# Attention scores that contract over one head's 64 rows, in a macaron block (MoE, attention, MoE) on one core

## The chip, the core and the metric

The kernel runs on one core of one Trainium2 chip. The core has five engines that run their own instruction streams and meet at semaphores: PE (TensorE, matmuls; its weight loads are shown apart as PEld), DVE (VectorE), ACT (ScalarE), POOL (GpSimd) and SP (SyncE, which here only issues DMAs). The metric is the device time of one execution in microseconds (us).

## What is computed

The reference, cut to what matters here:

```python
x = x + 0.5 * ffn(layernorm(x))       # mixture of 8 experts, 2 per token
x = x + attention(layernorm(x))
x = x + 0.5 * ffn(layernorm(x))       # the same weights again

def attention(h):                      # h: 4 x 512 x 256, 16 heads of 16 columns
    q, k, v = split(h @ w_qkv.T)
    scores = q @ k.T / sqrt(16)                        # per batch and head: 512 x 512
    scores = where(causal, scores, finfo.min)
    return (softmax(scores) @ v) @ w_o.T
```

The change touches the attention alone, and the tables that its causal masks read.

## The kernel before

The program is three phases in a row, `feed_forward` ("first"), `attention` and `feed_forward` ("second"), each with its own block of five hand-written instruction streams. The change is in `attention` and in `Constants.fill`, which POOL runs at the very start.

**Units.** Attention works in 8 units: 4 batches times 2 halves of 8 heads (`UNIT_HEADS`). `unit_loop` runs `front` for the first unit alone, and then 8 `step`s. In each step one unit's exponentials and values are made (`key_scores`, `exps`, `values`), and beside them the front of the next unit: its projections (`project`), the transposes that make its stacks (`turn`), and its scores for the row maxima (`scores`, `maximum`). The list `BESIDE` says by hand which part of the next unit's front stands behind which of the 16 `key_scores` calls (8 heads, two halves each); `VALUES_AFTER`, `OUTPUTS_AFTER` and `PROJECT_AFTER` place the rest. The last step has no next unit, so it has no scores.

**Stacks.** To reach float32 accuracy with fast matmuls, each head's q and k are split into a high and a low part and stacked: one head takes 64 contraction rows (three products of 16 rows, and two rows for the maximum). A transpose of 128 x 128 turns two heads at once, so a pair of heads lies in `q_stack` one above the other: the even head in partitions 0 to 63, the odd head in 64 to 127. A matmul here always reads all 128 partitions. So that the other head of the pair adds nothing, `k_stack` has two copies of the key columns (its second index, 0 or 1), each with the other head's half zero. The zeros are written once by POOL (L925); ACT copies each transposed block in two instructions of 64 partitions (`turn`, L986), one into each copy.

**Scores.** `scores` (PE, L1261) makes the queries-by-keys scores of one query tile. Query tiles 0 and 1 take two neighbouring heads in one bank (`SCORES`), tiles 2 and 3 one head. Each score matmul is followed by a bfloat16 matmul of 128 columns that adds the causal mask to the diagonal block: identity times `hide_later` (L1263). DVE then reduces the bank to row maxima (L1091 for two heads, L1095 for one). `key_scores` (L1289) makes the transposed scores that ACT's exponential reads (L1000); only the unit's last head has mask matmuls there (L1291), the others are cleared by POOL after the exponential.

**Banks and waits.** `project`, `turn` and `scores` share three PSUM banks in turn (`use`); a use waits until DVE or ACT has read the one three before it. The first `key_scores` of a step waits for a DMA that writes the maxima into `q_stack` (`max_in`). `values` (L1306) multiplies into 32 output partitions at a time: four matmuls on four column blocks of the array.

Of the kernel before, what the change touches and what calls it, by code (L numbers as in the profile page):

```python
# [47 lines left out]
class Constants:  # L48


    def __init__(self, nc, enter):
        def sb(name, shape, dtype=F32):
            return enter(nc.sbuf_tensor(name, shape, dtype))

        self.identity = sb("identity", [P, P])
        self.identity_bf = sb("identity_bf", [P, P], BF16)
        self.earlier = sb("earlier", [P, P], BF16)
        self.ones = sb("ones", [P, P], BF16)
        self.lane = sb("lane", [P, P])
# [5 lines left out]
        self.hide_later = sb("hide_later", [P, P], BF16)  # L65
        self.hide_later_t = sb("hide_later_t", [P, P], BF16)

        self.filled = enter(nc.semaphore("filled"))
        self.ready = enter(nc.semaphore("tables_ready"))

    def fill(self, pool):

        for table, value in ((self.identity, 0.0), (self.identity_bf, 0.0), (self.earlier, 1.0), (self.ones, 1.0),
                             (self.not_first, 1.0), (self.hide_later, 0.0), (self.hide_later_t, 0.0)):
            pool.memset(table[:], value).then_inc(self.filled, 1)
# [7 lines left out]
        pool.wait_ge(self.filled, 12)  # L83
        for table in (self.identity, self.identity_bf):
# [12 lines left out]
        pool.wait_ge(self.filled, 18)  # L97
# [578 lines left out]
def attention(nc, const, x, stats, x_rows, out_rows, w_qkv, w_o, rows_stored):  # L676
# [27 lines left out]
    SCORES = [(qt, (h, h + 1)) for qt in (0, 1) for h in range(0, UNIT_HEADS, 2)]  # L704
# [54 lines left out]
    with ExitStack() as stack:  # L759
# [13 lines left out]
        k_stack = [sb(f"k_stack{i}", [P, 2, PAIRS, SEQ], F32R) for i in range(2)]  # L773
# [138 lines left out]
        def _(pool):  # L912
# [11 lines left out]
            for i in range(2):  # L924
                pool.memset(k_stack[i][:].rearrange("p a b c -> p (a b c)").bitcast(F32), 0.0).then_inc(k_ready, 1)  # L925
# [30 lines left out]
        def _(act):  # L956
# [23 lines left out]
            def turn(u, hh, t):  # L980
# [66 lines left out]
        def _(v):  # L1047
# [38 lines left out]
            def maximum(u, hh, n):  # L1086
# [3 lines left out]
                if len(heads) == 2:  # L1090
                    v.reduce_max(maxima[:, qt, :, heads[0] // 2],  # L1091
# [94 lines left out]
        def _(pe):  # L1186
# [62 lines left out]
            def scores(u, hh, n):  # L1249
# [30 lines left out]
            def key_scores(b, hh, i):  # L1280

                h, half = i // 2, i % 2
                q, k = q_stack[hh][:, h // 2, :], k_stack[hh][:, h % 2, h // 2, :]
                pe.wait_ge(exped, 2 * UNIT_HEADS * (2 * b + hh) + i + 1)
                for j, (kt, q0) in enumerate(KEY_TILES[2 * half:2 * half + 2]):
# [4 lines left out]
                    if here:  # L1290
                        last = pe.matmul(out[:, kt * P - q0:(kt + 1) * P - q0], const.identity_bf[:], const.hide_later_t[:],  # L1291
                                         start=False, stop=True)
# [127 lines left out]
```

## Time and profile before

| | us |
|---|---|
| median of 3 runs | 1012.59 |
| the three runs | 1010.59, 1012.59, 1016.1 |
| span of the profiled execution | 1011.8 |
| PE busy, of the span | 836.9 |
| attention, from its first transposes to its last output matmuls | about 348 to 672 on the span's clock |

The time of the profiled execution is given as its span, from the first to the last instruction; it lies 0.8 us under the median of the runs. Rows of a timeline give the start, the duration, the engine, the line, the operation, output <- inputs, the shape and the count of merged instructions. The end of a matmul (start plus duration) is modelled with its pipeline, so that two ends in a row tell how far apart two matmuls really finish. A row "x2" merges two.

### The profile page before, as it was taken

How to read it: one execution, taken by the hardware profiler on the slowest of the kernel's cores; microseconds unless marked ns; L12 is line 12 of the kernel's file. 1: busy time of each engine (PE TensorE's matmuls, PEld its weight loads, DVE VectorE, ACT ScalarE, POOL GpSimd, SP SyncE). 2: the span in 40 equal slices, each digit the busy share in tenths (PEclk: the TensorE clock that was granted, in tenths of full speed). 3: DMA queues.
4: the chain of work that ended last, by engine and by line, in shares of the span. 5: the costliest groups of instructions: out<-in, count | busy, mean ns of one | idle time of the engine just before them, and what ended most of it. 6: DMA issues, size and time to landing. Idle time of an engine off the chain costs nothing. (4 is left out here: it accounts for less than half of the span.)

```text
span 1011.8 us, 16585 instructions
## 1 busy us (share of the span) xinstructions
PE 836.9 (83%) x5884; PEld 736.3 (73%) x5884; DVE 493.9 (49%) x1038; ACT 413.6 (41%) x743; POOL 308.5 (30%) x388
## 2 busy tenths in 40 slices
PE   4459899889898167999999999854599898998993
PEld 2459899889897155777677667442499898998993
DVE  7734444344341377655775666245554244433530
ACT  3024444344342132665465555523054344433530
POOL 1162543444333500211221121100533345335232
PEclk9779899999999578999999999777799899998997
DMA  9053234423411400101102001022133442443211
GB/s 332 1 162 95 58 105 108 119 48 103 117 22 17 151 1 2 42 3 44 44 0 80 6 1 41 2 86 102 52 121 99 120 113 49 109 119 94 47 16 20
DMA packets 52553, 72.15 MB, mean 71 GB/s; under 512 B 6272, under 2 KB 44160, under 8 KB 52480
## 3 DMA queue, kind: packets, MB, share of 16 engines
q1 hardware_dynamic: 37152, 52.71, 15.3%
q0 software_dynamic: 15360, 18.90, 10.7%
q8 instruction: 25, 0.41, 0.2%
q14 instruction: 16, 0.13, 0.0%
HBM read 53.49 MB, written 18.87 MB: 72 GB/s over the span
## 5 line engine op out<-in xcount | busy, mean ns | idle before, releaser
L1000 ACT ACTIVATE at_probs<-at_ps_keys 128x896 f32<-128x896 f32 (+1 forms) x128 | 96.0, 759 | 86.7 <-PE at_ps_keys L1289 77.4
L561 DVE SCALAR_TENSOR_TENSOR second_h_lo<-second_ps_h,second_h_hi 128x320 fp32r<-128x320 f32 x128 | 62.9, 491 | 103.9 <-ACT second_h_hi L414 103.9
L561 DVE SCALAR_TENSOR_TENSOR first_h_lo<-first_ps_h,first_h_hi 128x320 fp32r<-128x320 f32 x128 | 62.9, 491 | 103.2 <-ACT first_h_hi L414 103.2
L660 PE MATMUL second_ps_o<-second_w_hi,second_h_hi 128*128 128x256 f32 x320 | 95.8, 299 | 17.2 <-ACT second_scaled L407 17.2
L340 POOL DMA_INDIRECT out_dram<-second_scaled,second_add_now x40 | 63.8, 1594 | 151.1 <-DMA out_dram<-second_scaled,second_add_now 105.2
L340 POOL DMA_INDIRECT after_first<-first_scaled,first_add_now x40 | 63.7, 1593 | 146.8 <-DMA after_first<-first_scaled,first_add_now 104.4
L660 PE MATMUL first_ps_o<-first_w_hi,first_h_hi 128*128 128x256 f32 x320 | 95.7, 299 | 14.6 <-ACT first_scaled L407 14.6
L660 PE MATMUL second_ps_o<-second_w_lo,second_h_hi 128*128 128x256 f32 x320 | 93.7, 293 | 0.0
L660 PE MATMUL first_ps_o<-first_w_lo,first_h_hi 128*128 128x256 f32 x320 | 93.7, 293 | 0.0
L660 PE MATMUL second_ps_o<-second_w_hi,second_h_lo 128*128 128x256 f32 x320 | 93.6, 293 | 0.0
L660 PE MATMUL first_ps_o<-first_w_hi,first_h_lo 128*128 128x256 f32 x320 | 93.5, 292 | 0.0
L1261 PE MATMUL at_ps<-at_k_stack,at_q_stack 128*128 128x256 f32 (+2 forms) x256 | 84.5, 398 | 2.6 <-ACT at_k_stack L986 1.4
L1289 PE MATMUL at_ps_keys<-at_q_stack,at_k_stack 128*128 128x256 f32 (+2 forms) x256 | 76.7, 386 | 11.0 <-DMA at_q_stack<-at_max_t 9.5
L414 ACT ACTIVATE second_h_hi<-second_ps_h 128x320 fp32r<-128x320 f32 x128 | 56.0, 437 | 60.0 <-PE second_ps_h L649 60.0
L414 ACT ACTIVATE first_h_hi<-first_ps_h 128x320 fp32r<-128x320 f32 x128 | 55.9, 437 | 59.5 <-PE first_ps_h L649 59.5
L1095 DVE TENSOR_REDUCE at_maxima<-at_ps 128x1 f32<-128x512 f32 (+1 forms) x128 | 71.8, 617 | 16.8 <-PE at_ps L1263 16.4
L660 PEld LDWEIGHTS second_ps_o<-second_w_hi,second_h_hi 128*128 128x128 f32 x320 | 64.9, 203 | 18.2 <-ACT second_scaled L407 18.2
L660 PEld LDWEIGHTS first_ps_o<-first_w_hi,first_h_hi 128*128 128x128 f32 x320 | 64.7, 202 | 15.6 <-ACT first_scaled L407 15.6
L943 POOL TENSOR_SCALAR_AFFINE_SELECT at_probs<-at_probs 128x512 f32<-128x512 f32 (+1 forms) x64 | 35.3, 577 | 127.7 <-ACT at_probs L1000 127.7
L1289 PEld LDWEIGHTS at_ps_keys<-at_q_stack,at_k_stack 128*128 128x128 f32 x256 | 43.2, 203 | 32.7 <-ACT at_probs L1000 16.0
L660 PEld LDWEIGHTS second_ps_o<-second_w_lo,second_h_hi 128*128 128x128 f32 x320 | 64.9, 203 | 0.0
L660 PEld LDWEIGHTS first_ps_o<-first_w_lo,first_h_hi 128*128 128x128 f32 x320 | 64.8, 203 | 0.0
(266 smaller groups left out, 2033.1 us busy)
## 6 DMA issues: line engine op xcount, KB each, us to landing
first_w_raw<-in_L_ffn_w_dram SPq DMA_DIRECT2D x16, 1024.0 KB, 8.0
second_w_raw<-in_L_ffn_w_dram SPq DMA_DIRECT2D x16, 1024.0 KB, 6.7
at_xt<-at_xt_all SPq DMA_DIRECT2D x3, 1024.0 KB, 4.8
x<-_attn_hidden_states_dram SPq DMA_DIRECT2D x4, 512.0 KB, 5.8
normed_rows<-first_xn SPq DMA_DIRECT2D x4, 512.0 KB, 6.7
x<-after_first SPq DMA_DIRECT2D x4, 512.0 KB, 7.2
at_x_now<-after_first SPq DMA_DIRECT2D x4, 512.0 KB, 5.2
out_dram<-x SPq DMA_DIRECT2D x4, 512.0 KB, 3.2
```

Of the source, the lines that this page charges most:

```text
L340: pool.indirect_dma_start(sum_rows, bass.IndirectOffsetOnAxis(ap=add_now[par][:, s:s + 1], axis=0), scaled[par][:, s, :], None, bounds_che ...
L414: act.activation(h_hi[:, f, a * HALF:(a + 1) * HALF], ps_h[:, f % 2, a, 0:HALF], ACT.Relu).then_inc(h_hi_done, 1)
L561: v.scalar_tensor_tensor(h_lo[:, f, a * HALF:(a + 1) * HALF], ps_h[:, f % 2, a, 0:HALF], 0.0, h_hi[:, f, a * HALF:(a + 1) * HALF].bitcast( ...
L660: last = pe.matmul(ps_o[:, (par + s) % 2, 0:D], h[:, f, cs], w[par][:, f, :], start=(f == 0 and n == 0), stop=(f == FT - 1 and n == 2))
L943: pool.affine_select(probs[g][:, 0:heads, at:at + P], probs[g][:, 0:heads, at:at + P], [[0, heads], [1, P]], ALU.is_ge, 0.0, base=0, chann ...
L1000: act.activation(probs[h // GROUP][:, h % GROUP, columns], keys_columns(half), ACT.Exp, scale=float(HD) ** -0.5).then_inc(exped, 1)
L1095: v.reduce_max(maxima[:, qt, h % 2, h // 2:h // 2 + 1], bank[:, 0:(qt + 1) * P], AX_X).then_inc(front_kept, 1)
L1261: pe.matmul(out, q_stack[hh][:, h // 2, qt * P:(qt + 1) * P], k_stack[hh][:, h % 2, h // 2, 0:keys], start=True, stop=False)
L1289: last = pe.matmul(out, k[:, kt * P:(kt + 1) * P], q[:, q0:SEQ], start=True, stop=not here)
```

## The change

- `k_stack` loses its second index: the even head's keys stand in partitions 0 to 63 and the odd head's in 64 to 127, as in `q_stack`. ACT fills it with one copy of 128 partitions (`turn`) in place of two of 64. POOL's clearing writes 2048 columns in place of 4096.
- Score and key-score matmuls name the head's 64 partitions of both operands. In the built program they have a tile of [64, 128] of the array, at row 0 or row 64; before, they had [128, 128]. The columns that stream through are as many as before.
- A mask is two bfloat16 matmuls with 64 contraction rows, on the same rows as the head: `pick` and `hide_half` (`hide_half_t` for the key scores), each half of what the identity and the mask table did. The tables are filled at the start by 12 selects of 64 partitions in place of 2 of 128, and 3 memsets in place of 2.
- Where two heads share a bank, they are now of the same parity (0 and 2, 1 and 3, ...).

```diff
-                             (self.not_first, 1.0), (self.hide_later, 0.0), (self.hide_later_t, 0.0)):
+                             (self.not_first, 1.0), (self.pick, 0.0), (self.hide_half, 0.0), (self.hide_half_t, 0.0)):
...
-        pool.affine_select(self.hide_later[:], self.hide_later[:], [[-1, P]], ALU.is_ge, NEG, base=0,
-                           channel_multiplier=1).then_inc(self.filled, 1)
-        pool.affine_select(self.hide_later_t[:], self.hide_later_t[:], [[1, P]], ALU.is_ge, NEG, base=0,
-                           channel_multiplier=-1).then_inc(self.filled, 1)
+        HALF_ROWS = P // 2
+        for half in range(2):
+            rows = slice(half * HALF_ROWS, (half + 1) * HALF_ROWS)
+            pool.wait_ge(self.filled, 17 + 6 * half)
+            for part in range(2):
+                at = part * HALF_ROWS
+                pool.affine_select(self.pick[rows, part, :], self.pick[rows, part, :], [[-1, P]], ALU.not_equal, 1.0, base=at,
+                                   channel_multiplier=1).then_inc(self.filled, 1)
...
-    SCORES = [(qt, (h, h + 1)) for qt in (0, 1) for h in range(0, UNIT_HEADS, 2)]
+    SCORES = [(qt, (h, h + 2)) for qt in (0, 1) for h in (0, 1, 4, 5)]
...
-        k_stack = [sb(f"k_stack{i}", [P, 2, PAIRS, SEQ], F32R) for i in range(2)]
+        k_stack = [sb(f"k_stack{i}", [P, PAIRS, SEQ], F32R) for i in range(2)]
...
-                for odd in range(2):
-                    rows = slice(odd * STACK, (odd + 1) * STACK)
-                    last = act.activation(k_stack[hh][rows, odd, :, at],
-                                          front_bank(TURN[t] + 1)[rows, :].rearrange("p (a c) -> p a c", c=P), ACT.Copy)
-                last.then_inc(k_turned, 1)
+                act.activation(k_stack[hh][:, :, at], front_bank(TURN[t] + 1).rearrange("p (a c) -> p a c", c=P),
+                               ACT.Copy).then_inc(k_turned, 1)
...
-                    pe.matmul(out, q_stack[hh][:, h // 2, qt * P:(qt + 1) * P], k_stack[hh][:, h % 2, h // 2, 0:keys],
+                    rows = slice(h % 2 * STACK, (h % 2 + 1) * STACK)
+                    pe.matmul(out, q_stack[hh][rows, h // 2, qt * P:(qt + 1) * P], k_stack[hh][rows, h // 2, 0:keys],
                               start=True, stop=False)
-                    last = pe.matmul(out[:, qt * P:(qt + 1) * P], const.identity_bf[:], const.hide_later[:], start=False, stop=True)
+                    for part in range(2):
+                        last = pe.matmul(out[:, qt * P:(qt + 1) * P], const.pick[rows, part, :], const.hide_half[rows, part, :],
+                                         start=False, stop=(part == 1))
```

In PE's stream of a step, behind the first two key scores of a head, before (key scores L1289, the transposes of `turn` L1244, a projection L1213, scores L1261, mask L1263):

```order
L1289 MATMUL at_ps_keys<-at_q_stack,at_k_stack 128x512
L1289 MATMUL at_ps_keys<-at_q_stack,at_k_stack 128x384
L1244 MATMUL at_ps<-identity,at_row_stack 128x128 x8
L1289 MATMUL at_ps_keys<-at_q_stack,at_k_stack 128x256 x2
L1213 MATMUL at_ps<-at_w_hi,at_xt 128x384
...
L1213 MATMUL at_ps<-at_w_hi,at_xt 128x384
L1261 MATMUL at_ps<-at_k_stack,at_q_stack 128x256
L1263 MATMUL at_ps<-hide_later,identity_bf 128x128
L1261 MATMUL at_ps<-at_k_stack,at_q_stack 128x256
```

and now (the same with the line numbers of the changed kernel: L1300, L1251, L1220, L1269, L1272):

```order
L1300 MATMUL at_ps_keys<-at_q_stack,at_k_stack 128x512
L1300 MATMUL at_ps_keys<-at_q_stack,at_k_stack 128x384
L1251 MATMUL at_ps<-identity,at_row_stack 128x128 x8
L1300 MATMUL at_ps_keys<-at_q_stack,at_k_stack 128x256 x2
L1220 MATMUL at_ps<-at_w_hi,at_xt 128x384
...
L1220 MATMUL at_ps<-at_w_hi,at_xt 128x384
L1269 MATMUL at_ps<-at_k_stack,at_q_stack 128x256
L1272 MATMUL at_ps<-hide_half,pick 128x128 x2
L1269 MATMUL at_ps<-at_k_stack,at_q_stack 128x256
```

No work changed its place; the mask is doubled, and the rows of key scores and scores, which stand between transposes and projections of 128 rows, now have 64 rows.

On ACT, behind the first exponential (L1000) of the first step, before (copy of the keys L986, row stack L975):

```order
L1000 ACTIVATE at_probs<-at_ps_keys 128x896
L986 ACTIVATE at_k_stack<-at_ps 64x4x128 x2
L1000 ACTIVATE at_probs<-at_ps_keys 128x512
L975 ACTIVATE at_row_stack<-at_ps 128x16x16
L977 ACTIVATE at_v_ones<-at_ps 128x8x16
```

and now:

```order
L1007 ACTIVATE at_probs<-at_ps_keys 128x896
L994 ACTIVATE at_k_stack<-at_ps 128x4x128
L1007 ACTIVATE at_probs<-at_ps_keys 128x512
L985 ACTIVATE at_row_stack<-at_ps 128x16x16
L987 ACTIVATE at_v_ones<-at_ps 128x8x16
```

The second exponential of a head and the next projection's copies stand one copy nearer.

## Rows read from the trace of the kernel before

**Rows 1.** The page: span, then busy time and share of PE, then its 40 slices.

```profile
span 1011.8 us, 16585 instructions
...
PE 836.9 (83%) x5884; PEld 736.3 (73%) x5884; DVE 493.9 (49%) x1038; ACT 413.6 (41%) x743; POOL 308.5 (30%) x388
...
PE   4459899889898167999999999854599898998993
```

**Rows 2.** Stretches: length, PE, PEld, DVE, ACT, POOL busy (instructions), clock, DMA, GB/s.

```profile
412.00:640.00 228.00, 218.59 (x1658) 157.88 (x1656) 147.79 (x313) 130.11 (x228) 43.57 (x104) 1.00 0.08 28
357.00:397.00 40.00, 30.07 (x150) 23.12 (x150) 32.96 (x99) 10.75 (x26) 2.11 (x8) 0.86 0.00 1
```

**Rows 3.** Waits in 412 to 640: who for whom, us in total, times, longest.

```profile
PE at_ps_keys L1289 <- DMA at_q_stack<-at_max_t: 4.5, 6, 1.0
...
PEld at_ps L1261 <- DVE at_q_stack L1083: 3.1, 6, 0.8
PEld at_ps L1244 <- DVE at_row_stack L1077: 2.2, 3, 0.7
PEld at_ps L1261 <- ACT at_k_stack L986: 1.8, 11, 0.2
```

**Rows 4.** PE's timeline, 433 to 440: start us, duration us, instruction.

```profile
432.53 1.16 PE L1306 MATMUL at_ps_pv<-at_probs,at_v_ones 128*32 128x384 f32 x20
433.62 0.44 PE L1213 MATMUL at_ps<-at_w_hi,at_xt 128*128 128x384 f32 x1
...
434.42 0.33 PE L1213 MATMUL at_ps<-at_w_lo,at_xt 128*128 128x384 f32 x1
434.60 0.34 PE L1213 MATMUL at_ps<-at_w_hi,at_xt 128*128 128x384 f32 x1
...
438.60 0.33 PE L1213 MATMUL at_ps<-at_w_hi,at_xt 128*128 128x384 f32 x1
438.77 0.56 PE L1289 MATMUL at_ps_keys<-at_q_stack,at_k_stack 128*128 128x512 f32 x2
```

**Rows 5.** PE's timeline, 458.2 to 461.9, about the last values of a unit.

```profile
458.07 0.23 PE L1263 MATMUL at_ps<-hide_later,identity_bf 128*128 128x128 bf16 x1
458.23 0.43 PE L1306 MATMUL at_ps_pv<-at_probs,at_v_ones 128*32 128x128 f32 x8
458.58 0.67 PE L1289 MATMUL at_ps_keys<-at_q_stack,at_k_stack 128*128 128x512 f32 x2
459.10 0.40 PE L1261 MATMUL at_ps<-at_k_stack,at_q_stack 128*128 128x512 f32 x1
459.33 0.23 PE L1263 MATMUL at_ps<-hide_later,identity_bf 128*128 128x128 bf16 x1
459.37 0.48 PE L1261 MATMUL at_ps<-at_k_stack,at_q_stack 128*128 128x512 f32 x1
459.69 0.23 PE L1263 MATMUL at_ps<-hide_later,identity_bf 128*128 128x128 bf16 x1
```

**Rows 6.** PE's timeline, 33.5 to 34.2, in the first phase.

```profile
33.74 0.29 PE L611 MATMUL first_ps_x<-first_taken_bf,earlier 128*128 128x128 bf16 x1 [5.76 <-DVE first_before_bf L491]
33.82 0.31 PE L612 MATMUL first_ps_x<-first_before_bf,ones 128*128 128x128 bf16 x1
```

**Rows 7.** POOL's timeline at the start of attention.

```profile
344.83 6.98 POOL L925 MEMSET at_k_stack<- 128x4096 f32 x2
```

**Rows 8.** DVE's timeline at the start of attention.

```profile
346.77 1.60 DVE L130 TENSOR_SCALAR at_variance<-at_moments 128x4 f32<-128x4 f32 x1
...
349.25 2.60 DVE L142 TENSOR_SCALAR at_scratch<-at_scratch 128x4 f32<-128x4 f32 x1
```

**Rows 9.** Groups of ACT in 412 to 640: count, busy us, mean ns, idle before.

```profile
L986 ACT ACTIVATE at_k_stack<-at_ps 64x512 fp32r<-64x512 f32 x52 | 30.8, 593 | 2.1 <-PE at_ps L1244 1.8
```

**Rows 10.** POOL's timeline, start of the program: the last mask table.

```profile
4.12 0.29 POOL L95 TENSOR_SCALAR_AFFINE_SELECT hide_later_t<-hide_later_t 128x128 bf16<-128x128 bf16 x1
```

**Rows 11.** PE's timeline, 10 to 11: its first transposes.

```profile
10.68 0.66 PE L599 MATMUL first_ps_h<-identity,first_xn 128*128 128x128 f32 x2 [10.68 <-DVE first_xn L148]
```

More of the change, by code:

```diff
@@ L64, in __init__ @@
         self.not_first = sb("not_first", [P, E, T])
-        self.hide_later = sb("hide_later", [P, P], BF16)
-        self.hide_later_t = sb("hide_later_t", [P, P], BF16)
+        self.pick = sb("pick", [P, 2, P], BF16)
+        self.hide_half = sb("hide_half", [P, 2, P], BF16)
+        self.hide_half_t = sb("hide_half_t", [P, 2, P], BF16)
         self.filled = enter(nc.semaphore("filled"))
@@ L81, in fill @@
         pool.iota(self.token1[:], [[0, K], [P, T]], base=1, channel_multiplier=1, **small).then_inc(self.filled, 1)
-        pool.wait_ge(self.filled, 12)
+        pool.wait_ge(self.filled, 13)
         for table in (self.identity, self.identity_bf):
@@ L91, in fill @@
                            channel_multiplier=0).then_inc(self.filled, 1)
-        pool.affine_select(self.hide_later[:], self.hide_later[:], [[-1, P]], ALU.is_ge, NEG, base=0,
-                           channel_multiplier=1).then_inc(self.filled, 1)
-        pool.affine_select(self.hide_later_t[:], self.hide_later_t[:], [[1, P]], ALU.is_ge, NEG, base=0,
-                           channel_multiplier=-1).then_inc(self.filled, 1)
-        pool.wait_ge(self.filled, 18)
+        HALF_ROWS = P // 2
[6 more added lines that the diff above has]
+                                   channel_multiplier=1).then_inc(self.filled, 1)
+                pool.affine_select(self.hide_half[rows, part, :], self.hide_half[rows, part, :], [[-1, P]], ALU.is_ge, NEG,
+                                   base=at, channel_multiplier=1).then_inc(self.filled, 1)
+                pool.affine_select(self.hide_half_t[rows, part, :], self.hide_half_t[rows, part, :], [[1, P]], ALU.is_ge, NEG,
+                                   base=-at, channel_multiplier=-1).then_inc(self.filled, 1)
+        pool.wait_ge(self.filled, 29)
         pool.sem_inc(self.ready, 1)
@@ L924, in _ @@
             for i in range(2):
-                pool.memset(k_stack[i][:].rearrange("p a b c -> p (a b c)").bitcast(F32), 0.0).then_inc(k_ready, 1)
+                pool.memset(k_stack[i][:].rearrange("p a c -> p (a c)").bitcast(F32), 0.0).then_inc(k_ready, 1)
             def front(b, hh):
@@ L1090, in maximum @@
                 if len(heads) == 2:
-                    v.reduce_max(maxima[:, qt, :, heads[0] // 2],
+                    v.reduce_max(maxima[:, qt, heads[0] % 2, heads[0] // 2:heads[0] // 2 + 2],
                                  bank.rearrange("p (a c) -> p a c", a=2)[:, :, 0:(qt + 1) * P], AX_X).then_inc(front_kept, 1)
@@ L1282, in key_scores @@
                 h, half = i // 2, i % 2
-                q, k = q_stack[hh][:, h // 2, :], k_stack[hh][:, h % 2, h // 2, :]
+                rows = slice(h % 2 * STACK, (h % 2 + 1) * STACK)
+                q, k = q_stack[hh][rows, h // 2, :], k_stack[hh][rows, h // 2, :]
                 pe.wait_ge(exped, 2 * UNIT_HEADS * (2 * b + hh) + i + 1)
@@ L1290, in key_scores @@
                     if here:
-                        last = pe.matmul(out[:, kt * P - q0:(kt + 1) * P - q0], const.identity_bf[:], const.hide_later_t[:],
-                                         start=False, stop=True)
+                        for part in range(2):
+                            last = pe.matmul(out[:, kt * P - q0:(kt + 1) * P - q0], const.pick[rows, part, :],
+                                             const.hide_half_t[rows, part, :], start=False, stop=(part == 1))
                 last.then_inc(keys_made, 1)
```

## The prediction

> **What bounds the kernel now.** I read the page first: PE is busy for 83% of the span, and in the slices of the attention after its start nearly every digit is a 9 [rows 1]. Then the stretches, since the change sits in attention alone. From 412 to 640 us, seven steps of about 33 us, PE is busy 218.6 of 228 us at the full granted clock (1.00, that is 2.4 GHz), while DVE is busy 148 and ACT 130 [rows 2]. The waits say the same: PE's longest single wait there is for the DMA of the maxima, 4.5 us in all, and what its weight loads wait for on DVE and ACT sums to 3.1 + 2.2 + 1.8 = 7.1 us [rows 3]. So in these seven steps a microsecond more on PE is nearly a microsecond more in the program. In the lone front, 357 to 397 us, it is DVE that is full (33 of 40 us) and PE that is not at its pace [rows 2]; what PE gets there as extra work is hidden behind DVE's reductions. The two expert phases are untouched; they start earlier or later with what stands ahead of them.
>
> **Start of the program (0).** The last mask table is done at 4.12 + 0.29 = 4.41 us [rows 10], PE first needs the tables at 10.68 us, when it is let go by DVE [rows 11]. Ten more selects at 0.29 us or less and one more memset end before 7.6 us. The cover is three microseconds; nothing is added.
>
> **Start of attention (-2.4 us).** POOL clears `k_stack` from 344.83 to 351.81, two memsets of 3.49 us [rows 7]. Two small DVE operations on 4 columns take 1.60 and 2.60 us, and the latter ends at 351.85, just when the second memset does; the first ends at 348.37, when the first memset does [rows 8]. DVE is held by POOL's memset, and the norm that everything waits for stands behind it. With half the columns the memsets end at about 344.83 + 3.49 = 348.3 us. The operation at 346.77 is held as long as before, now by the second memset; the one at 349.25 is free and takes about 0.17 us. That gives 2.4 us, and DVE, which is full in the lone front behind it, passes them on.
>
> The Trainium skill (SBUF — State Buffer, Who interferes with whom) says that a tensor_scalar of VectorE in a two-port mode and GpSimd exclude each other for a whole instruction; the trace agrees, with 2.60 us for four columns.
>
> **Changes of tile (+21.5 us).** This is the largest term. Before, only `values` leaves the full array, for column blocks of 32, and the rows show what this costs. A projection of 384 columns behind another one ends 0.19 us after it (434.94 against 434.75); behind values it ends 0.37 us later (434.06 against 433.69) [rows 4]. Two key scores of 512 and 384 columns end 0.40 us after a projection (439.33 against 438.93 [rows 4]), and 0.59 us after values (459.25 against 458.66 [rows 5]). Leaving a tile costs 0.18 to 0.19 us, about half of it the weight load that is no longer hidden behind the matmul ahead. Going in costs 0.12 us by the starts: the values start 0.16 us after a mask, a score 0.04 us after one [rows 5]; their loads of 32 columns are short, those of a score are not. So I take 0.19 us for a change between 128 rows and 64 rows in either direction, and 0.14 us behind a mask, where 0.05 of the load is exposed already. Whether a tile that is cut by rows behaves as one cut by columns no row shows: the bounds are 0 and 0.19.
>
> The count is from the program: a step of the second half-unit has 8 changes into the 64-row tile and 8 out of it that are new, one of the first half-unit 19, as its head transposes and output projections stand between scores. The first step counts with the former: 4 x 16 + 3 x 19 = 121. Seven of them follow the wait for the maxima, where the array is idle in any case, and 14 leave behind a mask: 100 x 0.19 + 14 x 0.14 = 21.0, with the rounding up to 0.195 that the ends allow 21.5 us. The last step has five more, where PE waits for exponentials; they cost nothing.
>
> The Trainium skill (TensorEngine Tiling, Key Properties) says that changing the tiling mode drains the engine, while changing the tile within a mode does not. The trace agrees for column blocks; for rows nothing here shows it. By the rule the sum is as above; without it the term is 0.
>
> **The second mask (+7.7 us).** 7 x 32 masks of scores and 8 x 4 of key scores are in steps where PE sets the pace, 256 in all (32 more are in the lone front, under DVE). The nearest row for a bfloat16 matmul behind another: their ends are 0.10 us apart at the half clock [rows 6], so about 0.05 us at the full one. Against it: a score behind a mask ends 0.29 us after it, behind a key score 0.25 us [rows 5], so 0.04 to 0.06 us of the weight load is exposed today; the next head mostly lies on the other 64 rows, and its load may run under two masks now. The ends are +0.10 us (nothing gains from the clock) and -0.06 us (load and second mask both hidden): +26 and -15 us. I take 0.03 us, nearer to the row of two masks than to the gain, 256 x 0.03 = 7.7 us.
>
> **Heads side by side (-2 us).** Four values matmuls on different column blocks run at the same time: eight take 0.43 us [rows 5]. Score matmuls on different halves of the rows may, too. But matmuls issue in order, and each score is followed by its own masks on the same rows, so only a key score followed by a score of the other parity can gain: three per step, some 0.1 us each, 7 x 3 x 0.1 = 2 us. The bounds are 0 and -5.
>
> **ACT and what is absorbed (-5 us).** A key copy takes 593 ns for 64 partitions [rows 9], and a wider one no more; 28 of these go from the seven steps, 16.6 us of ACT's 130. ACT is not the bound, so this pays only where PE waits for it or through it: out of the 7.1 us of waits above. The same 7.1 us also take up delay on PE, since scores wait for banks that DVE empties meanwhile. Together I take 5 of the 7.1 us; the bounds are 0 and -7.
>
> **Sum.** 0 - 2.4 + 21.5 + 7.7 - 2 - 5 = +19.8 us on a span of 1011.8, that is 1031.6, and 0.8 more by the median of the runs: 1032 us.
>
> **Rivals.**
> - *No drain between row tiles.* The change of 21.5 us falls away; what is left is -2.4 + 7.7 - 2 - 5 = -1.7 us: about 1011 us, no difference. For it: the rows show column blocks only.
> - *Overlap wins (the other side, faster).* One mechanism: PE takes the next head's weights, for the other 64 rows, while this head's scores stream, and its matmul starts under the masks. It decides if that load starts before the first mask does. Then each head gains 0.06 us and hides its second mask, and no change drains: -2.4 - 15 - 2 to 5 - 5 to 7 = -24 to -29 with both ends, about 987; with half the overlap 998. I write 995. Against it: before, no load stands ahead of a bfloat16 mask's own, and loads go in order. The Trainium skill (TensorE: Matmul & The Clock Gate, Part 3, The mechanism) says that a load overlaps a running matmul only where the row groups differ, which would favour this case. The trace differs: loads of the same 128 rows are hidden already: projections end 0.19 us apart where their 384 columns alone take 0.16 us at 2.4 GHz [rows 4].
> - *Each change of half drains, too.* Neighbouring heads alternate between rows 0 and 64, some 28 times a step. At 0.19 us this adds 7 x 28 x 0.19 = 37 us, and the overlaps go: about 1072 us.
> - *Fewer rows make a matmul shorter.* Then scores shrink by up to half; no row shows a matmul of fewer rows, so nothing speaks for it. Counted with the second rival.
>
> **Chances.** Forecast 0.64, with its own range of 1014 to 1050; no drain 0.15; overlap wins 0.09; every half drains 0.12. The range of 1004 to 1052 takes in the forecast with the bounds of its masks for the most part, and the case without a drain: 0.62 + 0.15 and a little of the others, near 0.8. A measurement here can tell 0.5%, 5 us, from no change. Faster than 1007.5: the overlap and a quarter of "no drain", 0.13. Slower than 1017.7: 0.61 of the forecast and the fourth rival, 0.74, rounded with the tails. Between: 0.13.
>
> **What would show it.** In the changed profile: a key score behind transposes or a projection ends about 0.2 us later than 0.40 us after it; the two masks end about 0.05 us apart; the next score's load starts with the second mask; steps last 36 to 37 us in place of 33 to 35; the operation of 2.60 us on DVE takes 0.17. If the two key scores still end 0.40 us after a projection, the largest term was wrong.

## The result: slower by 1.2%

The changed kernel takes 1023.6 us (median), the kernel before 1011.6 us beside it: ratio 1.0117, 95% interval 1.0092 to 1.0142, from four runs of each. The forecast was 1032 us in a range of 1004 to 1052. The direction held; the sum came out 8 us too high, and its terms are further off than that, in both directions.

The page of the changed kernel: span, busy times, PE's slices and the granted clock. They stand beside [rows 1].

```profile
span 1021.1 us, 17150 instructions
...
PE 856.0 (84%) x6172; PEld 738.1 (72%) x6172; DVE 490.6 (48%) x1038; ACT 397.7 (39%) x711; POOL 307.6 (30%) x399
...
PE   4559989889997278999999999865499888988993
...
PEclk9779999999999576999999999657789999999997
```

The stretches of [rows 2], and the waits in 412 to 640 us that answer [rows 3]:

```profile
412.00:640.00 228.00, 222.35 (x1874) 152.78 (x1874) 144.03 (x308) 116.71 (x201) 43.58 (x104) 1.00 0.09 29
357.00:397.00 40.00, 32.93 (x182) 24.95 (x182) 31.76 (x94) 8.43 (x22) 2.11 (x8) 0.71 0.00 1
```

```profile
PE at_ps_keys L1300 <- DMA at_q_stack<-at_max_t: 4.1, 6, 0.7
PEld at_ps L1269 <- DVE at_maxima L1098: 3.2, 14, 0.3
PEld at_ps L1269 <- DVE at_maxima L1102: 2.2, 7, 0.3
```

The waits for the stacks that DVE and ACT make have shrunk to 0.9 us (they were the 7.1 us of [rows 3]); weight loads now wait for banks that DVE is still reducing. In the lone front, the part of attention ahead of the first step, the clock has fallen from 0.86 to 0.71, where PE is busier than before.

**Where the time went.** The first transposes of the maxima (L1271 before, L1281 now) begin each step. From their starts, the start of the memset and the end of the last projection (us):

| | before | changed |
|---|---|---|
| start of program to memset (POOL's clearing) of `k_stack` | 344.8 | 345.7 |
| memset to first maxima (lone front) | 52.3 | 50.8 |
| step 1 | 33.6 | 34.8 |
| steps 2 to 7 | 204.1 | 208.2 |
| last step and finish | 38.7 | 44.6 |
| the rest | 338.3 | 336.9 |

By spans the difference is +0.9 - 1.5 + 1.2 + 4.1 + 6.0 - 1.4 = +9.3 us. The six steps which bound the kernel, and for which the forecast had some 19 us, give four; six come from the last step, for which it had none. The first and the last line are code that is the same but for the tables: in the fourteen profiles of this study the memset starts anywhere between 344.8 and 350.1 us, so the whole span is a blunter measure than the parts of attention.

Below, **steps 2 to 7** is this 204.1 and 208.2. Kernels whose steps are the same differ in it by up to 1.3 us.

**Changes of tile.** PE's timeline of the changed kernel, about the place of [rows 4]. Ends are start plus duration.

```profile
438.29 0.50 PE L1300 MATMUL at_ps_keys<-at_q_stack,at_k_stack 64*128 64x256 f32 x2
438.72 0.44 PE L1220 MATMUL at_ps<-at_w_hi,at_xt 128*128 128x384 f32 x1
...
439.69 0.34 PE L1220 MATMUL at_ps<-at_w_hi,at_xt 128*128 128x384 f32 x1
439.96 0.67 PE L1300 MATMUL at_ps_keys<-at_q_stack,at_k_stack 64*128 64x512 f32 x2
```

Two key scores end 0.60 us after a projection (440.63 against 440.03), 0.40 before; a projection ends 0.37 us after a key score (439.16 against 438.79), as it did only after values. A tile cut by rows is left and entered at the price of one cut by columns, about 0.2 us. The Trainium skill (TensorEngine Tiling, Key Properties) says that a change of mode drains TensorE, without a price; the trace agrees for rows, with 0.60 for 0.40 us.

**Two halves of rows at once.** The same timeline somewhat later:

```profile
457.54 0.39 PE L1300 MATMUL at_ps_keys<-at_q_stack,at_k_stack 64*128 64x256 f32 x1
457.54 0.49 PE L1269 MATMUL at_ps<-at_k_stack,at_q_stack 64*128 64x512 f32 x1
...
459.12 0.56 PE L1269 MATMUL at_ps<-at_k_stack,at_q_stack 64*128 64x512 f32 x2
459.46 0.35 PE L1272 MATMUL at_ps<-hide_half,pick 64*128 64x128 bf16 x4
```

A key score and a score start at 457.54 both. At 459.12 two scores start 0.17 us apart and their four masks follow, while the program has score, two masks, score, two masks. The weight loads show it too: both scores' loads run at once, and the masks' come behind them.

```profile
459.12 0.19 PEld L1269 LDWEIGHTS at_ps<-at_k_stack,at_q_stack 64*128 64x128 f32 x2
459.45 0.18 PEld L1272 LDWEIGHTS at_ps<-hide_half,pick 64*128 64x128 bf16 x4 [0.15 <-issue]
```

In steps 2 to 7, 99 pairs of neighbouring scores or masks start within 12 ns of each other; before, none do. The prediction had put down this overlap as 2 us, because "matmuls issue in order". Between the two halves of the rows they don't. Within one half no row here shows an order other than the program's.

**Accounts of the pairs.** For steps 2 to 7 I took for each matmul how long after the matmul ahead of it (by start) it ends, and summed this by what the two are (us; pairs in brackets). "Full array" is transposes and projections, "scores" are scores, key scores and masks:

| | before | changed | same half | one mask | grouped |
|---|---|---|---|---|---|
| full array to scores or back | 28.2 (107) | 40.2 (107) | 40.9 (107) | 40.7 (107) | 33.4 (89) |
| among scores and masks | 78.2 (522) | 70.7 (738) | 74.4 (738) | 64.4 (522) | 70.0 (747) |
| with values | 41.1 (414) | 41.1 (414) | 41.3 (414) | 43.9 (414) | 41.1 (414) |
| full array among itself | 55.8 (438) | 56.0 (438) | 57.2 (438) | 58.1 (438) | 58.4 (447) |

The changes of tile cost 12.0 us net; scores and masks take 7.5 us less, although 216 masks were added. The last three columns are experiments, below.

**Start of attention.** POOL and DVE, answering [rows 7, 8]; the first projection starts 9.9 us after the memset instead of 12.3:

```profile
345.74 3.55 POOL L935 MEMSET at_k_stack<- 128x2048 f32 x2
```

```profile
347.72 1.59 DVE L140 TENSOR_SCALAR at_variance<-at_moments 128x4 f32<-128x4 f32 x1
...
350.19 0.17 DVE L152 TENSOR_SCALAR at_scratch<-at_scratch 128x4 f32<-128x4 f32 x1
```

**The last step.** Stretches of the kernel before and of the changed one, each from 9 to 30 us after the step's start:

```profile
643.90:664.90 21.00, 16.83 (x103) 8.22 (x102) 1.63 (x4) 11.02 (x17) 4.37 (x8) 0.74 0.00 1
```

```profile
648.50:669.50 21.00, 18.32 (x76) 8.82 (x79) 1.37 (x3) 10.78 (x16) 4.37 (x8) 0.50 0.00 1
```

The clock column is the thing to see: 0.50 is 1.2 GHz. In both kernels it falls some 6 us into the step; of these 6 us PE was busy for 4.0 and 4.1, with waits for exponentials, for the outputs and for the maxima between. Before, it is back at 1.00 (2.4 GHz) about 20 us into the step; now only 33 us into it, and 76 matmuls lie in a stretch that held 103.

### The profile page after: what moved, and what is told of

It reads as the page before. It is cut to its first block and busy times, and to the rows that moved or that the text cites. A ratio compares the mean times of both kernels' runs of the same rounds, so it can differ in the third digit from the quotient of the medians.

```text
span 1021.1 us, 17150 instructions
## 1 busy us (share of the span) xinstructions
PE 856.0 (84%) x6172; PEld 738.1 (72%) x6172; DVE 490.6 (48%) x1038; ACT 397.7 (39%) x711; POOL 307.6 (30%) x399
## 5 line engine op out<-in xcount | busy, mean ns | idle before, releaser
L1300 PE MATMUL at_ps_keys<-at_q_stack,at_k_stack 64*128 64x256 f32 (+2 forms) x256 | 80.9, 398 | 9.5 <-DMA at_q_stack<-at_max_t 8.0
L1269 PE MATMUL at_ps<-at_k_stack,at_q_stack 64*128 64x256 f32 (+2 forms) x256 | 83.0, 421 | 2.3 <-DVE at_maxima L1102 0.8
L1300 PEld LDWEIGHTS at_ps_keys<-at_q_stack,at_k_stack 64*128 64x128 f32 x256 | 42.1, 200 | 38.7 <-ACT at_probs L1007 16.7
```

Source lines behind the costliest of these rows:

```text
L1269: pe.matmul(out, q_stack[hh][rows, h // 2, qt * P:(qt + 1) * P], k_stack[hh][rows, h // 2, 0:keys], start=True, stop=False)
L1300: last = pe.matmul(out, k[:, kt * P:(kt + 1) * P], q[:, q0:SEQ], start=True, stop=not here)
```

## Experiments

Lengths, in us, for all kernels (m to m: memset to first maxima; "rows" are those of scores / key scores in the steps). The lengths are those of one profiled execution each. The runs were made in four sets, each with the kernel before beside it (medians of 1011.6 to 1015.8 us), so whole times are compared by their ratios and not by medians of different sets:

| kernel | rows | m to m | step 1 | 2 to 7 | last | ratio to before (95%) |
|---|---|---|---|---|---|---|
| before | 128 / 128 | 52.3 | 33.6 | 204.1 | 38.7 | |
| changed | 64 / 64 | 50.8 | 34.8 | 208.2 | 44.6 | 1.0117 (1.0092 to 1.0142) |
| wide memset | 64 / 64 | 54.6 | 39.2 | 209.4 | 44.8 | 1.0132 (1.0100 to 1.0165) |
| two copies | 64 / 64 | 52.6 | 38.1 | 210.7 | 44.8 | 1.0187 (1.0138 to 1.0236) |
| last full | 64 / 64, last step's keys 128 | 56.0 | 38.9 | 211.6 | 37.4 | 1.0173 (1.0120 to 1.0226) |
| late only | late 64 | 52.4 | 35.2 | 204.0 | 36.1 | 0.9998 (0.9976 to 1.0020) |
| same half | 64 / 64 | 53.6 | 35.8 | 214.0 | 44.8 | 1.0179 (1.0138 to 1.0219) |
| one mask | 64 / 64 | 50.4 | 33.9 | 207.6 | 37.5 | 1.0059 (1.0030 to 1.0089) |
| scores only | 64 / 128 | 56.0 | 34.9 | 209.2 | 36.8 | 1.0096 (1.0059 to 1.0133) |
| keys only | 128 / 64 | 52.3 | 40.0 | 222.4 | 44.7 | 1.0244 (1.0201 to 1.0287) |
| clock kept | 64 / 64, lone front and last step 128 | 52.7 | 34.7 | 210.8 | 38.7 | 1.0108 (1.0078 to 1.0138) |
| grouped | 64 / 64 | 51.9 | 35.0 | 203.1 | 44.8 | 1.0022 (1.0000 to 1.0043) |
| memset pieces | 128 / 128 | 52.1 | 33.6 | 204.5 | 37.0 | 0.9996 (0.9978 to 1.0014) |
| late pieces | late 64 | 52.7 | 35.2 | 204.3 | 33.9 | 0.9973 (0.9951 to 0.9994) |

### The memset and the copies

```diff
-                pool.memset(k_stack[i][:].rearrange("p a c -> p (a c)").bitcast(F32), 0.0).then_inc(k_ready, 1)
+                pool.memset(k_wide[i][:].rearrange("p a b c -> p (a b c)").bitcast(F32), 0.0).then_inc(k_ready, 1)
```

> The changed kernel, but POOL clears a buffer of 4096 columns twice, as the kernel before did, of which keys use the first half. If the memset's hold on VectorE is the gain at the start of attention, the second small VectorE operation takes about 2.6 us again (0.17 in the changed kernel), the first projection comes 2.4 us later against the memset's start, and the whole is about 2 us longer than the changed kernel (0.2%). The rival is that the gain came from something else there: then the operation stays at 0.17 us and the time stays. For the last step: if scores on 64 rows hold TensorE's clock low, the granted clock is 0.50 from some 5 us after the last maxima to the end of attention here as well, and that step is 44 us long; if it was chance in one profiled execution, it is near 38 us.

DVE's timeline of this kernel:

```profile
347.25 1.58 DVE L140 TENSOR_SCALAR at_variance<-at_moments 128x4 f32<-128x4 f32 x1
...
349.70 2.60 DVE L152 TENSOR_SCALAR at_scratch<-at_scratch 128x4 f32<-128x4 f32 x1
```

2.60 us are back, and the first projection is 12.3 us after the memset again. This term is shown, in place and size. The whole is 1.5 us longer by the ratios, near the 2 us expected, but their intervals overlap widely. In the profile it is more, 9.6 us from the memset to the end of attention: step 1 took 39.2 us for 34.8, at a mean clock of 0.79 for 0.90, and two later steps had 0.97 and 0.98 for 1.00. Nothing in those steps differs between the two kernels, so the clock of a step can differ by that much with the same instructions, and the lengths of step 1 in the table say little about the rows. The last step is 44.8 us long once more, so its length was not chance in a single profile.

```diff
-                act.activation(k_stack[hh][:, :, at], front_bank(TURN[t] + 1)..., ACT.Copy).then_inc(k_turned, 1)
+                for odd in range(2):
+                    rows = slice(odd * STACK, (odd + 1) * STACK)
+                    last = act.activation(k_stack[hh][rows, :, at], front_bank(TURN[t] + 1)[rows, :]..., ACT.Copy)
```

> The changed kernel with ScalarE's one copy of the keys of 128 partitions split into two of 64 partitions again (28 more copies of 0.59 us in the seven steps, 16.6 us). The prediction gave the saved copies up to 5 us, together with what waits absorb. By that the time is 2 to 5 us longer than the changed kernel. The rival: ScalarE is nowhere waited for long, and the saving is worth nothing: within 1 us of it, with the steps at 34.8 and 33.0 us alternately. Last step: low clock to its end (44 us) if 64 rows are the cause, near 38 us if it was chance.

Steps 2 to 7 rise from 208.2 to 210.7 us. Two more kernels with the same steps and two copies have 210.8 and 211.6, the two with one copy 208.2 and 209.4: the single copy is worth about 2 us, in the scores and masks of the accounts (72.7 for 70.7 us). In the changed kernel it takes 598 ns, as [rows 9] had led me to expect:

```profile
L994 ACT ACTIVATE at_k_stack<-at_ps 128x512 fp32r<-128x512 f32 x26 | 15.5, 598 | 2.9 <-PE at_ps L1251 0.2
```

### Are the two halves served apart?

```diff
-    SCORES = [(qt, (h, h + 2)) for qt in (0, 1) for h in (0, 1, 4, 5)]
-    SCORES += [(qt, (h,)) for qt in (2, 3) for h in range(UNIT_HEADS)]
+    SCORES = [(qt, (h, h + 2)) for qt in (0, 1) for h in (0, 4, 1, 5)]
+    SCORES += [(qt, (h,)) for qt in (2, 3) for h in (0, 2, 4, 6, 1, 3, 5, 7)]
```

> The changed kernel with the heads' scores in another order: neighbouring scores lie on the same 64 rows (heads 0, 2, 4, 6, then 1, 3, 5, 7) where they alternate now; number of matmuls, masks and changes between 64 and 128 rows stay. Theory A (the two halves of the rows are served independently, and the overlap of neighbours pays back what drains and masks cost): most of the overlap is gone, and steps two to seven, 208.2 us together in the changed kernel, are 8 to 24 us longer; the scores' starts are no longer 7 ns behind another's. Theory B (matmuls start in order, and alternation gives next to nothing, as the prediction had it with 2 us): within 2 us of 208.2. Theory C (a change of half costs a drain as well): shorter by some us, down to 180.

214.0 us, 5.8 more than 208.2: theory B and C fall, and A holds in direction, though its 8 us was too much. 63 of the 99 coincident starts are left, since a key score still often has a neighbour in the other half. The accounts put 3.7 of the 5.8 us among scores and masks; 1.2 lie among full-array work, where nothing changed but the clock (0.98 in two steps), so some 4.5 us are the order's: in the four steps at the full clock it costs 0.74 to 0.80 us each.

> The changed kernel without the second of the two mask matmuls, so that keys that come later are hidden for half of a diagonal block's rows only. Steps two to seven hold some 220 of these matmuls. The prediction's price, 0.03 us each, makes these steps 6.6 us shorter than 208.2 (201.6); the full 0.056 us that one takes behind another where nothing else runs, 12.3 us (196); if the halves are independent and the second mask of a head runs beside the next head's work, 0 to 5 us (203 to 208).

```diff
-                    for part in range(2):
-                        last = pe.matmul(out[:, qt * P:(qt + 1) * P], const.pick[rows, part, :], const.hide_half[rows, part, :],
-                                         start=False, stop=(part == 1))
+                    last = pe.matmul(out[:, qt * P:(qt + 1) * P], const.pick[rows, 0, :], const.hide_half[rows, 0, :],
+                                     start=False, stop=True)
```

This kernel hides later keys for half of a diagonal block's rows only, so it does not compute the attention. Steps 2 to 7 are only 0.5 us shorter, as if the second masks were hidden, but here this sum misleads: the clock was below 1.00 in four of the six steps (0.93 to 0.97; two of them are even longer than in the changed kernel, 37.4 and 34.1 us against 36.7 and 33.0), which lengthens the last two lines of its accounts, where nothing was changed. In the two steps at the full clock it is 0.9 and 1.0 us shorter. The stretch that holds the six steps, of this kernel and of the changed one:

```profile
432.40:640.00 207.60, 201.67 (x1483) 136.27 (x1481) 128.75 (x278) 105.84 (x185) 39.18 (x96) 0.97 0.08 27
```

```profile
431.40:639.50 208.10, 202.66 (x1699) 139.62 (x1697) 129.14 (x278) 105.74 (x185) 39.16 (x96) 1.00 0.08 27
```

Among scores and masks 216 matmuls fewer take 6.3 us less, 0.029 us each, and the two steps at the full clock say much the same (0.9 to 1.0 us for 36 masks). That is the price that was forecast. Behind each other with nothing beside them two masks end 0.056 us apart; about half of that is covered.

So beside the 7.5 us that scores and masks save stand some 6 us that the added masks cost: 14 us are gained there, where the prediction had 2. This 14 is what is left over, not measured by itself. Of it about 2 us go with the single copy and some 4 with the order of the heads (3.7 in these lines); the rest is put down to the overlap by the coincident starts.

> Zero half and two copies as before; row scores on 64 rows with two masks, key scores on 128 rows with one. To be compared with the kernel that has two copies and 64 rows throughout: its steps two to seven take 210.7 us. Theory A (halves independent): a key score can no longer lie beside a row score, and every group of row scores is fenced by drains on both sides, 11 groups in a step and so 6 changes more than there; these steps are longer by 6 x 6 x 0.19 = 7 us and the lost overlap, together 10 to 20 us. Theory B (the gain came from 64-row scores as such, not from lying side by side): only the 7 us of drains. Clock in the last step: 128-row key scores bring it back, the step is 36 to 39 us, not 44.

> The mirror of the former: zero half and two copies as before, key scores on 64 rows with two masks, row scores on 128 rows with one. Theory A (halves independent): no neighbours on different halves but the key scores of one head and the next, so nearly all overlap is lost and the drains are paid; steps two to seven come to 218 to 232 us against 210.7. Theory B: only the drains, near 218. Clock: in the lone front 128-row scores keep it up, so the first maxima come near 399 us as with 128 rows throughout and not at 401 to 403; in the last step, with 64-row key scores alone, it stays at 0.50 and the step takes 44 us.

```diff
+                    full = SCORES_FULL(n)                          # scores only: False, keys only: True
+                    rows = slice(0, P) if full else slice(h % 2 * STACK, (h % 2 + 1) * STACK)
...
+                full = KEYS_FULL(i, b is LAST and hh == 1)         # scores only: True, keys only: False
```

Their steps 2 to 7, in this order:

```profile
436.17:645.40 209.23, 202.07 (x1676) 142.63 (x1674) 130.66 (x278) 118.00 (x211) 39.33 (x96) 1.00 0.08 27
```

```profile
438.30:660.70 222.40, 217.75 (x1508) 147.29 (x1507) 131.50 (x278) 119.69 (x209) 39.17 (x96) 1.00 0.08 25
```

Scores alone on 64 rows cost 5.2 us against before, key scores alone 18.3, both together (two copies) 6.6. So 16.9 us are had only when both are on 64 rows: the overlap of one with the other, and the changes between them that fall away. These runs do not part the two. The expectation for the first was wrong by 10 us or more: I had counted six more changes between 64 and 128 rows in a step, but the trace holds 132 in the six steps (values included) against 155, and 120 coincident starts against 99, since scores still lie beside scores. Key scores on 64 rows have 179 changes and no coincident start, as theory A has it.

### The clock

> Keys in a buffer with a zero half and two copies, scores and keys on 64 rows with two masks as in the changed kernel, but the key scores of the last step alone (the one with no next unit beside it) read 128 rows with one mask, as before. If 64-row scores are what keeps the granted clock at 0.50 in that step, it comes back near 12 us before the step's end, values take about 2.4 us for 32, and the step is about 38 us instead of 44; the whole is then some 6 us shorter than the changed kernel, less 2.4 us for the wider memset and what the two copies cost. If the clock there is chance or has another cause (what comes ahead of the step), the step stays near 44 us.

> Zero half and two copies as before. The scores of the lone front and the key scores of the last step read 128 rows with one mask; everything in the steps between, where the next unit's work stands beside the key scores, reads 64 rows with two masks. Clock theory (64-row scores that stand alone do not bring the granted clock back to 1.00): lone front and last step go as with 128 rows, so from the memset to the first maxima 52.4 us (54.6 and more with 64 rows and the same memset), last step 36 to 39 us and not 44.7; steps two to seven stay at 210.7 us as with two copies throughout. The whole is then 8 to 10 us below the kernel with two copies and 64 rows throughout, near 1021 us. Rival (the low clock comes from where a step happens to begin, whatever the rows): front and last step fall on either side, and one of them shows 54 or 44 us.

```diff
+                    full = u is FIRST and hh == 0                  # clock kept; last full: False
...
+        return last_step                                           # key scores on 128 rows in the last step, both kernels
```

The last step is 37.4 and 38.7 us, where the six kernels with 64-row key scores and two masks there have 44.6 to 44.8. Its middle (9 to 30 us after its start) in the kernel with 128 rows there alone, and in the one with two copies and 64 rows:

```profile
662.30:683.30 21.00, 15.91 (x104) 7.37 (x104) 2.06 (x5) 10.49 (x16) 4.38 (x8) 0.84 0.00 1
```

```profile
658.50:679.50 21.00, 18.32 (x76) 8.81 (x78) 1.37 (x3) 10.69 (x16) 4.38 (x8) 0.50 0.00 1
```

Over all profiles: with 128-row key scores in the last step the clock's mean there is 0.73 to 0.95 in seven of seven; with 64 rows it is 0.50 in six of seven. The seventh is the kernel with one mask: it fell to 0.50 like the others and came back (0.70, step of 37.5 us). Its key scores have 64 rows too, so it is the clock and not the rows by themselves that makes the step long. 64 rows go with the low clock, but something else, perhaps the missing masks or when the step begins, has a say; that stays open.

In the lone front there is a split as well. Its last 21 us before the first maxima, for the kernel before, the one with clock kept (128-row scores in the front), the changed one, and the one with scores only (64 rows there, both):

```profile
376.20:397.20 21.00, 17.27 (x91) 12.15 (x92) 19.03 (x42) 4.89 (x9) 0.00 (x0) 0.92 0.00 1
```

```profile
381.10:402.10 21.00, 18.97 (x90) 13.69 (x90) 18.85 (x41) 4.84 (x9) 0.00 (x0) 0.76 0.00 1
```

```profile
375.60:396.60 21.00, 20.25 (x111) 14.12 (x107) 17.54 (x38) 2.99 (x5) 0.00 (x0) 0.59 0.00 1
```

```profile
380.30:401.30 21.00, 20.64 (x103) 14.56 (x104) 17.24 (x37) 3.58 (x6) 0.00 (x0) 0.50 0.00 1
```

Four profiles with all scores there on 128 rows have 0.76 to 0.92, and eight with all on 64 rows 0.50 to 0.59, although PE is busier in these. The kernels late only and late pieces lie between, with 0.78 and 0.74: they have 64 rows for query tiles 2 and 3 in the lone front too, 16 of the 28 scores in this stretch. The added masks are not the cause, since the kernel with one mask has 0.52; why 64 rows go with a low clock is not shown. DVE, busy for 19.0 of 21 us before, is busy for 17.5. The clock kept kernel is 9.3 us shorter than two copies from memset to the end of attention (336.9 against 346.1), 6.1 of it in the last step, 3.4 in step 1 (which is not the rows' doing: the changed kernel, on 64 rows, has 34.8 us there for the 34.7 here), and nothing in the front, where the wider memset takes the 2.4 us that the clock gives. The expected whole, near 1021 us, was missed (1026.6): its first phase was 1.3 us later, and the rest of the program 2.1 us longer. By the ratios, 1.0108 for 1.0187, it is 8 us below two copies, as expected.

### Fewer changes, and versions for both

> The changed kernel with its first two pairs of row turn and projection side by side after key scores 0 and 2, instead of one after each of key scores 0 to 3. In steps two to seven this takes 18 of the 107 changes between full-array work and scores away. If each costs 0.13 to 0.19 us, as the accounts of the pairs give, these steps come to 204.7 to 205.9 us from 208.2. Rival (TensorE then waits for the copies of these banks by VectorE and ScalarE, which had a key score's time before): 208 to 211 us.

```diff
-    BESIDE = [[("turn", 0)], [("project", 2)], [("turn", 1)], [("project", 3), 0, 1],
+    BESIDE = [[("turn", 0), ("project", 2)], [], [("turn", 1), ("project", 3)], [0, 1],
```

203.1 us, 5.1 less, more than expected and less than the kernel before has. The account across the array falls by 6.8 us with 18 changes fewer and that among full-array work rises by 2.4 with the pairs that moved there; no wait took the place. That is 0.28 us for each change that fell away, more than the 0.13 to 0.19 expected; what the rest is stays open. With this order the change costs 0.2% (interval 0 to 0.4%), though in the profile attention is still 6.0 us longer than before (334.7 against 328.7), and its last step is 44.8 us long as ever. Whether the kernel before would gain from this order too was not run.

> 128 rows and one mask for the scores of query tiles 0 and 1 (n below 8), for the first seven key groups and in the whole last step; 64 rows and two masks only for the scores of query tiles 2 and 3, which stand side by side with key scores late in a step. Theory 1 (row halves run independently, the changes of tile and the masks eat the gain): most of the overlap is kept and many of the changes of tile go, so steps come to 32 to 34 us, and the whole to 995 to 1008 us, faster than before. Theory 2 (matmuls issue in order, as the prediction had it; the steps gained elsewhere): the steps are no shorter than before's 33.6 and 32.7 to 35.7 us, the whole is 1011 to 1020 us.

```diff
     def SCORES_FULL(n):
+        return n < 8
     def KEYS_FULL(i, last_step):
+        return last_step or i < 7
```

Theory 2 came nearer: 204.0 us in steps 2 to 7, no difference to the kernel before. Changes take 2.0 us more, scores and masks 1.6 less; the overlap that is left (47 coincident starts) and its price are even. Theory 2 had this length because matmuls issue in order, which the starts contradict; it was nearer in number alone.

> The kernel before, with each of the two memsets of the key buffers written as four of 1024 columns (0.87 us each, the same 7 us in all). If VectorE's small operations are held to the end of the POOL instruction that runs, they are held for under 0.9 us each instead of 1.6 and 2.6, and the first projection comes 2.5 to 3.5 us earlier against the first memset (12.27 us before): about 1009 us against 1011.6. Rival (the pieces follow so closely that VectorE gets no turn between them): the operations are held as long as before, and the time stays.

```diff
-                pool.memset(k_stack[i][:].rearrange("p a b c -> p (a b c)").bitcast(F32), 0.0).then_inc(k_ready, 1)
+                flat = k_stack[i][:].rearrange("p a b c -> p (a b c)").bitcast(F32)
+                for piece in range(4):
+                    last = pool.memset(flat[:, piece * 1024:(piece + 1) * 1024], 0.0)
+                last.then_inc(k_ready, 1)
```

DVE's timeline:

```profile
352.13 0.74 DVE L130 TENSOR_SCALAR at_variance<-at_moments 128x4 f32<-128x4 f32 x1
...
353.75 0.93 DVE L142 TENSOR_SCALAR at_scratch<-at_scratch 128x4 f32<-128x4 f32 x1
...
354.91 3.19 DVE L148 TENSOR_SCALAR x<-x,at_moments,at_inverse 128x256 f32<-128x256 f32 x4
```

The holds are as short as expected, 0.74 and 0.93 us. But the norm itself now runs while POOL still clears, and its four operations together take 3.19 us, not the 1.38 of an idle POOL. The first projection is only 0.6 us earlier, the time the same. A hold was shortened and another one met.

> The kernel with 64 rows only for scores of query tiles 2 and 3 and the key scores beside them, and its memsets in four pieces each as well. Its six steps took 204.0 us with whole memsets, the kernel before 204.1, so with pieces I expect 2.5 to 3.5 us less than it, 1008 to 1010 us, and no difference to the kernel before with pieces. If row halves beside each other were a gain of their own here, it would be some us below that one.

0.9973 (0.9951 to 0.9994) is the only ratio below 1 with its whole interval, by 0.3% and barely. Its steps 2 to 7 (204.3) gain nothing; it is the last step, 33.9 us at a clock of 0.95, that makes attention 2.6 us shorter in the one profile, with the same 128-row key scores there as in the kernel before. With twelve kernels compared, a gain as small as this can be chance; I would not call it a better kernel.

## Why the prediction was right and where it was not

- **Direction and range: right**, with the expected largest cost. **The size** was 20 us for a measured 12. That it came so near owes something to luck: an overlap that was missed, a clock that was missed and changes that arrived only in part cancel for the most part.
- **Start of program (0): right.** First transposes at 10.87 us for 10.68. **Start of attention (-2.4): right**, and undone by the wide memset.
- **Changes of tile (+21.5): the mechanism and the price were right.** By the pairs, a score behind a transpose ends 0.19 us later after it than before, a projection behind a key score 0.20, a projection behind a mask 0.14. Of the some 18 us that this makes in six steps, 12.0 arrive. The rest fell, at least in part, on waits that were there before, as the separate term of -5 said: at six places a score of 256 columns ended 0.61 us behind a projection before and ends 0.31 us behind it now, 1.8 us in all. **ACT** alone gave about 2 us.
- **The second mask (+7.7): right**, 0.029 us each against 0.03, though not for the reason given: the next score's load does not start with the second mask but ahead of the first, and about half of the mask's 0.056 us runs beside the other half's work.
- **Heads side by side (-2): the step that failed**, by its bound of -5 as well. In its place stand about -14 us in six steps (what is left over in the accounts, with some 2 us of the single copy in it). "Matmuls issue in order, and each score is followed by its own masks on the same rows" is what the timeline contradicts. The second rival had the mechanism, and its sign, the next head's load ahead of the first mask, stands in the rows at 459.12, but it took the drains away with it. That each change of half drains, the third rival, is out by the same rows and by the order of the heads (+4.5 us where halves alternate less). A matmul of fewer rows is not shorter, as the fourth had it: a key score of 384 columns behind another ends 0.175 us after it before and 0.176 now. The Trainium skill (TensorE: Matmul & The Clock Gate, Part 3, The mechanism) holds matmuls to program order as well; the rows at 459.12 differ.
- **The last step (0): failed**, +6.0. I counted its changes and its waits, and not the clock at which PE comes out of them. The same is true of the lone front, where work on PE was to be "hidden behind DVE's reductions": at 0.59 PE is busy for 20.25 of 21 us there, and DVE waits, so that of the 2.4 us of the memset 1.5 are left at the first maxima.
- **Steps of 36 to 37 us: half right.** Steps 3, 5 and 7, with output projections, take 36.7, 36.7 and 35.6 us (35.7, 35.4 and 34.9 before), steps 2, 4 and 6 take 33.0 (32.7).

## What to carry to other kernels

Price a change of the contraction rows both ways: each passage between 64-row and full-array work costs 0.14 to 0.2 us, and in return neighbours on different halves run at once, which only happens where such work stands next to each other. Move full-array work together first (5 us here for one line). Here the gain never came out clearly above the price. Look separately at stretches in which the engine waits much: there the granted clock can set the time, as it did in this last step.

## What the runs showed of the hardware

- Matmuls on rows 0 to 63 and 64 to 127 start at the same time and overtake each other: 457.54 and 457.54 us, and two scores ahead of the first one's masks. Putting more neighbours on the same half costs some 4.5 us in six steps.
- With all scores on 64 rows the clock has a mean of 0.50 to 0.59 in the last 21 us of the lone front (eight profiles), with all on 128 rows 0.76 to 0.92 (four), mixed 0.74 and 0.78 (two), although PE is busy for longer at 64 rows. In the middle of the last step it is 0.50 in six of seven profiles with 64-row key scores, and 0.73 to 0.95 in seven of seven with 128-row ones.
- A VectorE operation on four columns is held by POOL's memset for what is left of the instruction (2.60 or 0.93 us; 0.17 when POOL is idle), and four VectorE operations of 256 columns take 3.19 for 1.38 us beside memsets of 0.9 us.
